# A blocked Chebyshev and hyperbolic graph kernel: seven half-size products for eight in its third sweep

## The reference

```python
def L0(h, adj, weight, bias):            # Chebyshev, K = 4
    T0, T1 = h, adj @ h
    out = T0 @ weight[0] + T1 @ weight[1]
    for k in (2, 3):
        T = 2.0 * (adj @ T1) - T0
        out = out + T @ weight[k]
        T0, T1 = T1, T
    return out + bias

def L1(h, adj, kernel, bias):
    support = adj @ poincare_expmap(h, 1.0)
    return poincare_logmap(support, 1.0) @ kernel + bias

h = relu(layernorm(x));  x = x + L0(h, adj, L0_weight, L0_bias)
h = relu(layernorm(x));  x = x + L1(h, adj, L1_kernel, L1_bias)
```

## Time and profile before

| | us |
|---|---|
| median of 3 runs | 1854.42 |
| lowest and highest | 1854.24, 1854.57 |
| the profiled execution's own time | 1854.24 |
| its span, first to last instruction | 1852.4 |
| matrix engine busy | 1830.2 (99%) |
| vector engine busy | 413.7 (22%) |
| scalar engine busy | 121.3 (7%) |
| GpSimd busy | 41.1 (2%) |
| moved by DMA | 662.31 MB, 358 GB/s over the span |

### The profile page before, as it was taken

The page is one execution under the profiler, slowest core; times in us unless marked ns, Lnnn a source line. Parts: engine busy times, 40 slices in busy tenths (PEclk is TensorE's granted clock), DMA queues, the critical chain, the costliest instruction groups (busy, mean ns, idle before and its releaser), DMA issues.

```text
span 1852.4 us, 22385 instructions
## 1 busy us (share of the span) xinstructions
PE 1830.2 (99%) x9620; PEld 825.3 (45%) x9620; DVE 413.7 (22%) x853; ACT 121.3 (7%) x233; POOL 41.1 (2%) x65
## 2 busy tenths in 40 slices
PE   7999999999999999999999999999999999999997
PEld 4444444444444445444444444344444444444444
DVE  7111111111122123000000001532321222122136
ACT  1000000000000000000000000311000000000014
POOL 0000000000000000000000000000000000000003
PEclk9999999999999999999999999999999999999998
DMA  9999999999999986888888785899999999999995
GB/s 379 421 421 421 421 420 416 387 394 389 399 371 381 374 331 228 319 295 298 295 302 304 263 303 208 331 379 377 372 383 395 384 377 382 407 384 384 406 397 202
DMA packets 94833, 662.31 MB, mean 358 GB/s; under 512 B 11408, under 2 KB 13712, under 8 KB 14608
## 3 DMA queue, kind: packets, MB, share of 16 engines
q1 hardware_dynamic: 93744, 660.64, 91.5%
q10 hardware_dynamic: 992, 0.23, 0.1%
HBM read 658.74 MB, written 2.10 MB: 357 GB/s over the span
## 4 chain that ended last, share of the span: by engine, by line
PE 97%; DVE 1%; DMA 1%; SPq 0%; issue 0%; ACT 0%; DVEq 0%
PE row_bank L523 36%; PE work_bank L503 19%; PE work_bank L537 17%; PE row_bank L492 12%; PE row_bank L525 4%; PE own_bank L553 3%; PE work_bank L505 3%; PE turned L608 2%; DMA ring<-adj_blocks 1%; PE work_bank L577 0%; SPq L417 0%; PE own_bank L564 0%; PE own_bank L608 0%; PE row_bank L608 0%; SPq L428 0%
## 5 line engine op out<-in xcount | busy, mean ns | idle before, releaser
L525 PE MATMUL row_bank<-ring,nodes 128*64 128x512 f32 x1728 | 756.6, 592 | 0.0
L523 PE MATMUL row_bank<-ring,nodes 128*64 128x512 f32 x1728 | 756.6, 592 | 0.0
L523 PEld LDWEIGHTS row_bank<-ring,nodes 128*64 128x64 f32 x1728 | 236.4, 137 | 419.0 <-issue 416.2
L505 PE MATMUL work_bank<-ring,nodes 128*64 128x512 f32 x936 | 420.8, 592 | 0.0
L503 PE MATMUL work_bank<-ring,nodes 128*64 128x512 f32 x936 | 420.8, 592 | 0.0
L537 PE MATMUL work_bank<-ring,nodes 128*64 128x512 f32 x1456 | 342.2, 592 | 0.3 <-DVE nodes L888 0.2
L492 PE MATMUL row_bank<-ring,nodes 128*64 128x512 f32 x1112 | 269.8, 596 | 6.2 <-DMA ring<-adj_blocks 6.2
L525 PEld LDWEIGHTS row_bank<-ring,nodes 128*64 128x64 f32 x1728 | 236.4, 137 | 0.0
L503 PEld LDWEIGHTS work_bank<-ring,nodes 128*64 128x64 f32 x936 | 127.9, 137 | 218.8 <-issue 218.8
L537 PEld LDWEIGHTS work_bank<-ring,nodes 128*64 128x64 f32 x1456 | 124.4, 137 | 169.6 <-issue 167.8
L784 DVE TENSOR_TENSOR partial<-partial,work_bank 128x512 f32<-128x512 f32 x148 | 101.7, 688 | 332.5 <-PE work_bank L537 331.4
(11 more groups left out here) (106 smaller groups left out, 518.4 us busy)
## 6 DMA issues: line engine op xcount, KB each, us to landing
ring<-adj_blocks SPq DMA_DIRECT2D x626, 1024.0 KB, 7.7
out<-resid SPq DMA_DIRECT2D x16, 128.0 KB, 1.9
resid<-x SPq DMA_DIRECT2D x7, 256.0 KB, 11.4
resid<-x SPq DMA_DIRECT2D x2, 128.0 KB, 3.5
w_raw<-cheb_weight ACTq DMA_DIRECT2D x2, 64.0 KB, 7.8
bias<-cheb_bias ACTq DMA_DIRECT2D x1, 32.0 KB, 2.8
bias<-hyp_bias ACTq DMA_DIRECT2D x1, 32.0 KB, 3.8
w_raw<-hyp_kernel ACTq DMA_DIRECT2D x2, 16.0 KB, 8.8
```

What stands on the lines that cost most here:

```text
L505: done = nc.tensor.matmul(bank[EVEN, :], nodes[:, c * C + k, B, :], data[:, k, :], start=k == 0, stop=k == C - 1)
L523: nc.tensor.matmul(bank[ODD, :], nodes[:, c * C + k, A, :], data[:, k, :], start=first and k == 0, stop=last and k == C - 1)
L525: done = nc.tensor.matmul(bank[EVEN, :], nodes[:, c * C + k, B, :], data[:, k, :], start=first and k == 0, stop=last and k == C - 1)
```

## The change

In the third sweep, for rows 6 to 15, a BOTH visit no longer makes 8 products of 64 features by 512 columns. The block is seen as 2 x 2 quarters (two chunks x 256 columns each), the features as 2 x 2 quarters too (two chunks x 32 features), and the product of the two is made with seven quarter products instead of eight (Winograd's form). A visit has 7 rounds of 4 products of 32 features by 256 columns, each in its own 32-column tile of the array (`tile_position=(0, lane)`).

For that:
- the vector engine makes four combinations of the block's quarters (`s_mixed`), two visits before the block is used; one overwrites a quarter in the ring, three go to SBUF space given up by five slots of the ring;
- GpSimd makes four combinations of the features of each row when they are known (`SUMS`), into the same space;
- the products of a row fill both row banks, so there is no second pair to alternate with. At a row's end the scalar engine copies out and swaps halves between partitions (five copies, `s_aside`), the vector engine joins the sums (`JOIN`, six operations), and the next row's first products wait for `s_aside` and `s_cleared`;
- from the start of level 4 until the last such visit only 8 slots of the ring take new blocks;
- for rows 8 to 14 the block (r,r-1) is a BOTH visit and no longer an OWN and an AGAIN visit, and the diagonal OWN visit comes last in the row (for row 15 both OWN visits come last);
- loads are ordered by first need, which for such a block is two visits before its own;
- OWN visits, AGAIN visits of level 4 and TURN of levels 3 and 4 use products of 32 features, so twice as many, with the same columns in all.

```diff
-SLOTS = 13
+SLOTS, KEPT_SLOTS = 13, 8
+FAST_FROM, LATE_FROM = 6, 8
...
+        if level == 3 and row >= FAST_FROM:
+            follow(2 if row < NB - 1 else 1, ("JOIN", row), lambda: None)
+            visits_to_turn = 5
...
-        return list(range(max(LOW, row + 1))) if row <= LOW else [row, row - 1]
+        return list(range(max(LOW, row + 1))) if row <= LOW else [row] if LATE_FROM <= row < NB - 1 else [row, row - 1]
...
-        return range(row - 1) if row > LOW else range(0)
+        return range(row if LATE_FROM <= row < NB - 1 else row - 1) if row > LOW else range(0)
...
-            for v in [("OWN", k, c) for c in own_columns(k)] + [("BOTH", k, c) for c in both_columns(k)]]
+            for v in [("OWN", k, c) for c in own_columns(k) if k < LATE_FROM] +
+            [("BOTH", k, c) for c in both_columns(k)] + [("OWN", k, c) for c in reversed(own_columns(k)) if k >= LATE_FROM]]
...
+    fast = [i for i in in_order if steps[i][0] == "BOTH" and phase_of[i] == 2 and steps[i][1] >= FAST_FROM]
...
+        needed_at[i] = in_order[in_order.index(i) - 2]
+        mix_before.setdefault(needed_at[i], []).append(i)
...
+        if last > shared_from:
+            for k in range(KEPT_SLOTS, SLOTS):
+                slot_free[k] = max(slot_free[k], shared_to)
...
+                    nc.gpsimd.tensor_tensor(sum_of(c, 0), features(c, 1, 0), features(c, 1, 1), ALU.add)
+                    nc.gpsimd.tensor_tensor(sum_of(c, 2), features(c, 0, 0), features(c, 1, 0), ALU.subtract)\
...
+                    nc.gpsimd.tensor_tensor(sum_of(c, 1), sum_of(c, 0), features(c, 0, 0), ALU.subtract)\
...
+                    nc.gpsimd.tensor_tensor(sum_of(c, 3), features(c, 0, 1), sum_of(c, 1), ALU.subtract)\
...
+                    elif first:
+                        pe.wait_ge(s_cleared, row)
+                        pe.wait_ge(s_aside, 5 * row)
...
+                    rounds = [(("A11", "B11", 0, high, N1), ("A11", "B11", 1, high, N1)),
+                              (("A12", "B21", 0, low, N1), ("S3", "T3", 0, low, N2)),
+                              (("A12", "B21", 1, low, N1), ("S3", "T3", 1, low, N2)),
+                              (("S4", "B22", 0, low, N2), ("S2", "T2", 0, high, N2)),
+                              (("S4", "B22", 1, low, N2), ("S2", "T2", 1, high, N2)),
+                              (("S1", "T1", 0, high, N2), ("A22", "T4", 0, low, N1)),
+                              (("S1", "T1", 1, high, N2), ("A22", "T4", 1, low, N1))]
+                    for k, pair in enumerate(rounds):
+                        if k in (1, 3, 5):
+                            pe.wait_ge(s_mixed, 4 * n + 1 + (k + 1) // 2)
+                        for part, (a, b, h, bank, columns) in enumerate(pair):
+                            for level in (A, B):
+                                lane = level * F + part * H
+                                done = nc.tensor.matmul(bank[lane:lane + H, columns], left(a, h, level), right[b][:, h, :],
...
-                        half = (ODD, EVEN)[k % 2]
-                        done = nc.tensor.matmul(bank[half, :], nodes[:, c * C + k, A, :], data[:, k, :],
-                                                start=first and k < 2, stop=last and k >= 2)
+                        for part in range(2):
+                            lane = k % 2 * F + part * H
+                            done = nc.tensor.matmul(bank[lane:lane + H, :],
+                                                    nodes[:, c * C + k, A, part * H:(part + 1) * H], data[:, k, :],
...
+                    size = F if level < 3 else H
...
-                        for half in (0, 1):
-                            part = slice(half * F, (half + 1) * F)
+                        for lane in range(0, P, size):
+                            part = slice(lane, lane + size)
...
+                    nc.scalar.activation(common[:, 1, :], row_banks[1][:, N2], ACT.Copy).then_inc(s_aside, 1)
+                    for lane in range(0, P, F):
+                        for to, come in ((0, H), (H, 0)):
+                            nc.scalar.activation(aside[lane + to:lane + to + H, :], row_banks[1][lane + come:lane + come + H, :],
...
+                for j in mix_before.get(i, []):
...
+                    dve.wait_ge(s_visit, visit_no[fast[n - 2]] if n >= 2 else shared_from)
+                    dve.wait_ge(s_landed[slot_of[load_of[j]]], uses_of[load_of[j]] * 16)
...
+                    nc.vector.tensor_tensor(mix_of(n, 0), block[:, 0:2, N2], block[:, 0:2, N1], ALU.subtract)\
...
+                    nc.vector.tensor_tensor(block[:, 0:2, N2], block[:, 2:4, N2], block[:, 0:2, N2], ALU.subtract)\
...
+                    nc.vector.tensor_tensor(mix_of(n, 1), block[:, 2:4, N2], mix_of(n, 0), ALU.subtract).then_inc(s_mixed, 1)
...
+                    nc.vector.tensor_tensor(mix_of(n, 2), block[:, 2:4, N1], mix_of(n, 1), ALU.subtract).then_inc(s_mixed, 1)
...
+                    dve.wait_ge(s_aside, 5 * row + 1)
+                    step(nc.vector.tensor_tensor(both, both, low[:, N2], ALU.add))
+                    step(nc.vector.scalar_tensor_tensor(joined[:, N1], both, second_half[:, 0:1], low[:, N1],
...
+                    dve.wait_ge(s_aside, 5 * (row + 1))
+                    nc.vector.tensor_tensor(joined[:, N2], both, aside[:, N2], ALU.add)
+                    nc.vector.tensor_tensor(own, high[:, N1], aside[:, N1], ALU.add).then_inc(s_cleared, 1)
```

168 lines of the change are left out of this document (145 added, 23 removed).

## The result

| | before | after |
|---|---|---|
| median, us | 1854.2 | 1859.0 |
| lowest and highest of 8 runs | 1853.7, 1855.2 | 1855.6, 1860.4 |
| the profiled execution's own time | 1854.24 | 1856.76 |
| its span | 1852.4 | 1854.6 |
| mean granted clock of its span | 0.996 | 0.994 |

The ratio is 1.0023, with a 95% interval from 1.0014 to 1.0032: slower by 0.23%. The forecast was 1849.1, faster. The runs of the kernel before agree within 1.5 us; those of the changed one spread over 5; the experiments come back to that.

A forecast was written before the change was run, and what follows sets the result against it. The prediction took the matrix engine, busy 99% of the span, as the bound. From 1854.4 us, -42.5 for the visits and +24.2, 4.1, 2.3, 4.3, 0.7 and 1.6 in costs gave 1849.1 us, range 1841 to 1864.

The forecast's parts named there:

- 102 visits: Rows 6 to 15: each seven-product visit takes 3.017 us instead of 3.434, saving 42.5 us in all.
- end of a row: Before rows 8 to 15 the matrix engine waits for the row banks, 3.9 us once and 2.9 seven times: +24.2 us.
- tail: Around row 15 the matrix engine waits 2.2 us for a work bank and 1.9 for features: +4.1 us.
- middle of a row: Rows 9 to 14: features 0.5 us late three times, 0.1 four times, combinations 0.2 late three times: +2.3 us.
- turns: TURN of levels 3 and 4 with twice the records takes longer: +4.3 us, bounds 0 to 8.6.
- tile shapes: Third sweep: nine changes between 64- and 32-column tiles cost +0.7 us, at worst 1.4.
- GpSimd: Its four feature operations per row delay the vector engine's combinations: +1.6 us over all rows, bounds 0 to 6.
- loads: Block loads fit a row with its wait, and eight slots hold some 15 us ahead: priced at 0.
- clock at a row's end: Rival, 3%: the clock falls after the row-end waits, all eight +13.6 us, 1863; not in the sum.
- the first rival: The change does what it says and turns and tile shapes cost nothing, GpSimd hidden: 1842.5 us, 18%.
- this rival: The vector engine is the bound, its combinations following at 0.69 us instead of 0.60: 1859 us, 15%.
- Four tiles are four: Answers a rival, 10%: four tiles not quite four, a new visit taking 3.17 us: 1862 us.

The follow-up runs named there:

- e4_tiles_of_32: The kernel before with OWN, AGAIN of level 4 and TURN of levels 3 and 4 in 32-column tiles, BOTH kept at 64; 1877.11 us in a single run.
- e6_no_sums: The changed kernel without GpSimd's four combinations of each row's features, products reading plain features; 1858.64 us, ratio 1.0023.
- e1_fill: The changed kernel with three or four rounds of idle matrix products in the waits before rows 8 to 15; 1852.21 us, ratio 0.9988.
- e2_cover3: The changed kernel with three AGAIN visits instead of one between rows, first combinations three visits ahead; 1839.91 us, ratio 0.9926.
- e3: The changed kernel without the vector engine's four combinations for each block, products reading plain quarters; 1853.29 us in a single run.
- e8_cover3_fill8: The changed kernel with three AGAIN visits between rows, plus four rounds of idle products before row 8 alone; 1840.29 us, ratio 0.9925.
- e9_fill_short: The changed kernel with one round of idle matrix products in each wait before rows 8 to 15; 1852.24 us, ratio 0.9993.
- e10_cover2: The changed kernel with two AGAIN visits instead of one between rows, first combinations three visits ahead; 1843.52 us, ratio 0.9949.

## Why the prediction went wrong

The profiled execution against the sum:

| term | forecast | measured | |
|---|---|---|---|
| 102 visits | -42.5 | -42.2 | 3.02 us each |
| end of a row | +24.2 | +24.7 | 23.3 idle, 0.17 more for each restart |
| tail | +4.1 | +4.6 | waits of 2.3 and 1.98, and their restarts |
| middle of a row | +2.3 | +5 | 4.0 idle in nine waits, 0.1 more for each restart |
| turns | +4.3 | -0.3 | 0.45 us for 32 records |
| tile shapes | +0.7 | +1.3 | nine at 0.14 (e4_tiles_of_32) |
| GpSimd | +1.6 | 0 | e6_no_sums |
| loads | 0 | 0 | no wait in this profile's sweep |
| clock at a row's end | 0 | +6.8 | four falls of 1.7 |
| first two sweeps | 0 | +0.9 | first TURN at 58.57 for 57.66 |
| sum | -5.3 | about +1 | |
| profile | | +2.5 | about 1.7 has no place |

**The step that failed is the clock.** The prediction knew the mechanism. It had the row, "idle 3.7 → clock at half for 3.4 us, 1.7 lost", and the other, an idle 1.62 without effect; it priced all eight falls at 13.6. Then it gave the case 3%, and put no fall in the sum. The waits that it forecast, one of 3.9 and seven of 2.9, lie nearer to 3.7 than to 1.62, and one of them lies beyond. By its own two rows the 3.9 should have been in the sum at 1.7, and the seven at anything from 0 to 11.9, of which the middle is 5.9. The sum would then have been 1849.1 + 7.6 = 1856.7, no faster than before, and the profile came to 1856.8. That close a fit is partly luck, since the other misses nearly cancel. The measured time lies in the range of 1841 to 1864, but the forecast went the other way: faster had 52%, slower 26%.

The 1.7 itself held, though the row that it was taken from didn't show a loss. That row is from the first 14 us of the span of the kernel before, and the products there are followed by a wait for a block, so the load would have hidden it:

```profile
16.69 1.94 PE L492 MATMUL row_bank<-ring,nodes 128*64 128x512 f32 x8 [1.33 <-DMA ring<-adj_blocks]
```

In the third sweep nothing hid it.

**Mis-sized terms.** *Turns*: the lower bound, "0.47 (four tiles at once)", was right, and four tiles made it 0.45; this is the first rival's mechanism. The middle was taken without a row for it, at a cost of 4.6. *Middle of a row*: the features come 0.5 late three times, as counted, but 0.29 late three times, not 0.1 four times; the combinations come 0.53 late three times, not 0.2. Where it missed, the count ran 0.2 to 0.3 us short. *GpSimd*: the bound of 0 held. *Eight slots*: in the old order they cost 2.9, not 0; in the changed kernel's profile no load is waited for in the third sweep, but in others 0.3 to 1.7 us in rows 6 and 7. *First sweeps*: 0.9 us are lost by the first TURN, before anything of the change runs. The first wait for a block is 4.7 us where it was 3.7; why is not explained. Up to TURN 3 it becomes 1.3, with three of the nine changes of tile shape.

**The other rivals.** The vector engine is not the bound: independent combinations follow each other at 0.60, not at 0.69. That this rival's 1859 is the measured median is luck, since nothing of its mechanism is seen. The vector engine's busy share between 1240 and 1760 is 76%, less than the 80% that the forecast itself had named as its sign; its other signs, rounds of 0.2155 and waits of 23.3 us at line 1016, came true. Four tiles are four: 28 products of 32 x 256 in 14 rounds of 0.2155. The loads don't set a row in the changed kernel (398 GB/s in 1350 to 1760), as its waits leave them room. With the waits covered they ran at 414 to 420 GB/s, so 393 is not the limit that the forecast had feared.

**What is left open.** Whether a wait of 2.8 us brings the clock down differs from wait to wait, and between builds: rows 8, 12, 14 and 15 in both profiles of the changed kernel, rows 8 to 12 in e6_no_sums. No experiment told what decides it. Nor is it settled why the median run of the changed kernel is 2.3 us above its profiled one. By the clocks of the runs one or two more falls would do it, but a run without a trace doesn't show where they are. Two other things that differ between the profiles would do it as well: a fall at 26 us of the span, which costs 1.8 us (below), and the waits for loads in rows 6 and 7, up to 1.7. About 1.7 us of the profiled time has no place in the table.

## What to carry over

Price a new wait on the matrix engine twice, once for its length and once for the clock behind it; here 1.7 us was added to a wait of 2.8 in about half of the cases, and a wait kept under 2 us at a row's end had no second price. Idle products in the gap bring the second price back, and useful visits bring back both, which made this change the fastest version of all once three visits stood between the rows (1839.9 us). Where a gain of 42 us meets a cost of 24, look first for how the cost can be covered, and then which limit comes next; here the loads, at 414 of 421 GB/s, are the likely one.

## What the runs showed of the hardware that was not expected

- **Idle length and clock.** Waits of the matrix engine at the row ends in the third sweep, in nine profiles (the changed kernel twice, e1 to e3, e6, e8 to e10):

| idle before the row, us | followed by half clock |
|---|---|
| 0.2 to 1.2 | none |
| 1.9 | 0 of 7 |
| 2.5 | 1 of 2 |
| 2.7 to 2.9 | 13 of 26 |
| 3.0 to 3.9 | 7 of 7 |

  Each fall lasted 3.4 us, in two cases 6.8. Length alone doesn't decide. The waits behind row 15, 2.3 us the longest, had no fall behind them in any of the nine. But at 25 us of the span, where the matrix engine had idled before as well, a wait of 2.0 to 2.2 us for the scalar engine's copy was followed by a fall in e1_fill and e9_fill_short, and not in the changed kernel's first profile and e10_cover2. In e1_fill, the wait, and the window behind it:

```profile
25.54 1.12 PE L719 MATMUL work_bank<-w_h,aside 128*64 128x64 f32 x16 [2.16 <-ACT aside L779]
```

```profile
25.50:29.00 3.50, 3.46 (x24) 1.75 (x25) 2.88 (x5) 0.17 (x1) 0.00 (x0) 0.51 1.05 429
```

  It cost 1.8 us: the first TURN starts at 60.37 where it is 58.57 in the changed kernel.
- **Small records on four tiles.** 32 records of 64 columns pass in 0.45 us, 0.014 each, where 16 on two tiles took 0.47, 0.029 each. With four tiles issue is no limit down to that.
- **A change between 64- and 32-column tiles** costs 0.14 us (e4_tiles_of_32, 22.8 us for 159).
- **The DMA beside a fully working core.** 420 GB/s over 60 us (e8_cover3_fill8) and 75 us (e2_cover3, 1565 to 1640) with the matrix engine busy 97 to 98% and the vector engine 77 to 78%, the same as in the slices of the first sweep, where the vector engine does little.
